# Gated values summed on VectorE head by head, in place of products on VectorE and sums on GpSimd

## The chip, the cores and the metric

The kernel runs on one core of one Trainium2 chip. The metric is the device time of one execution in microseconds (us), from the first to the last instruction and what lies around it. The engines are called as in the profile: PE is TensorE, DVE is VectorE, ACT is ScalarE, POOL is GpSimd, SP is SyncE.

## The reference

A stream x of 8 sequences of 512 tokens with 128 columns passes four layers, each added to the stream: attention with 16 heads, a mixture attention, another attention, and the same mixture again. Only the mixture's values matter here. It has 8 heads of 64 columns, and 5 experts; each head of each token picks two experts for its values:

```
gl_v = (x @ Ws).reshape(b, t, h, e)
wv = _topk_mask(gl_v, SEL) * jax.nn.sigmoid(gl_v)
xv = jnp.einsum('btd,edk->btek', x, Wv)
v = jnp.einsum('bthe,btek->bhtk', wv, xv)
scores = jnp.einsum('bhid,bhjd->bhij', q * scale, k)
probs = jax.nn.softmax(scores, axis=-1)
attn = jnp.einsum('bhij,bhjd->bihd', probs, v)
```

So the value of one head and token is a sum over the five experts of a gate times 64 columns that all heads share.

## The kernel before, in words

The two layers of each kind and the 8 sequences give 16 units of work. `iteration(j)` runs 19 times; it works on three units at once: unit j is prepared (normalised, projected), unit j-1 goes through attention A, and unit j-2 through the mixture F, whose last part falls into the iteration after. An iteration has 8 slots (0 to 3 for the four groups of attention heads, 4 to 7 for the four pairs of mixture heads) of up to 10 steps each; (slot, b) names a step. Each engine runs the same list of slots and steps in order, and semaphores (`Signal`) connect them. There is no planner: what stands at which step is written out by hand, in tables.

In slots 2 to 5 PE computes the scores of the mixture (L484), two of 512 columns at a time, into three banks S1a, S1b and S1c. For each, DVE takes the negative maximum (nmaxF, L991), and ACT the exponential (Pq, L805), which frees the bank for PE. Beside it, PE transposes or multiplies into S2 and ACT copies to PT; POOL masks PT in slots 0 to 3 (L1246).

The values of the mixture lie in `Vf` (128 tokens of each of NT = 4 token tiles i, 8 heads, 64 columns). They come from `xv` (the five experts' columns of a token tile) and the gates `wv_s`. `f_value_product(i, e)` (L1067) runs on DVE at the 20 steps of `V_STEPS` (L186), in the order of i and then e: one product of 512 columns for all eight heads (L1076), with both inputs spread by stride 0. For e = 0 it goes straight to `Vf`; for e = 1 to 4 it goes to one of four buffers in `ztmp`, and `f_value_sum` (L1264) on POOL adds it to `Vf` (L1271). `v_mult` counts products, `v_acc` counts sums. A product waits for the sum four before it, where the buffers go round. The last iteration with values, j = 17, has no attention beside it; there the steps are those of `V_LAST` (L189) and the buffers lie in `PT`.

PE reads `Vf` in slot 5 (`values`, L517, matmul L550), after a wait for the sums of the token tile. Four steps on other lines play a part: `rotate` (L954 and L960, DVE), `rest1` and `part2` (L1257 and L1261, POOL, which split the rotated tensor), and the sum of the residual with a bias into `res` (L1301, POOL), which stands at step (4, 8) behind DMA loads. `split_maxima` (L1004 and L1006, DVE) makes `nmb` at the start of slots.

Of the kernel before, what the change touches and what calls it, by code (L numbers as in the profile page):

```python
# [19 lines left out]
def attention_and_mixture(nc, x, wa, wp, ba, bv, bp, tab, wqk, wgv, wo, ident_in, mask_in, out):  # L20
# [47 lines left out]
    NF_B = GF * NT  # L68

    ctx = ExitStack()  # L70
    with ctx:
# [6 lines left out]
        class Signal:  # L78
# [76 lines left out]
        maskf = ztmp[:, 0, 0, 0:2, :].rearrange("p a b -> p (a b)")  # L155
        VBUF = 4
        vtmp = ztmp[:, :, :, :, :].rearrange("p b t e d -> p (b t e d)")[:, 0:VBUF * HF * DF].rearrange(
            "p (j h d) -> p j h d", j=VBUF, h=HF)
        S1 = [pb("S1a"), pb("S1b"), pb("S1c")]
# [79 lines left out]
        sig_e = Signal("sig_e", 1)  # L239
        v_mult = Signal("v_mult", NT * E)  # L240
        v_acc = Signal("v_acc", NT * (E - 1))
        z_mult = Signal("z_mult", HF)
# [62 lines left out]
        def mix_step(k, g, h):  # L305

            return (2, 5) if (k, g, h) == (UNITS + 1, 3, 1) else ((SA + g + 2) % NS, 2 * h + 1)

        def vtmp_of(k, n):

            return PT[:, n % VBUF // 2, NF_B + n % 2, :].rearrange("p (h d) -> p h d", h=HF) if k == UNITS + 1 else vtmp[:, n % VBUF, :, :]

# [111 lines left out]
        def _(pe):  # L424
# [7 lines left out]
            def iteration(j, a, f, f_end, a_prep, f_prep):  # L432
# [84 lines left out]
                def values(slot, kt):  # L517
# [26 lines left out]
                    else:  # L544
                        if kt == 0:
                            pe.wait_ge(exps_done.sem, exps_done.at(j, BEFORE2[slot]))
                        if group == SA:
                            pe.wait_ge(v_acc.sem, v_acc.at(j, (E - 1) * (kt + 1), 2))
                        for h in range(GF):
# [221 lines left out]
        def _(act):  # L771
# [6 lines left out]
            def iteration(j, a, f, f_end, a_prep, f_prep):  # L778
# [54 lines left out]
                def f_gates(i):  # L833
                    use = f"F gate{i}"
                    if i == 0:
                        act.wait_ge(v_mult.sem, v_mult.at(j, v_mult.per, 2))
                    act.wait_ge(*filled(j, use))
                    nc.scalar.activation(gate[:, :, i, :], bank(use)[:, 0:NG].rearrange("p (e g) -> p e g", e=E), ACT.Copy)
                    nc.scalar.activation(xv[:, i, :], bank(use)[:, NG:NG + NX], ACT.Copy).then_inc(is_free(use), 1)
# [66 lines left out]
        def _(dve):  # L906
            for s in (m0_drained, m1_drained, s1_read, maxF_ready, resA_ready, resF_ready, varA_ready, varF_ready, xnA_ready,
                      xnF_ready, rot_ready, nmb_ready, v_mult, z_mult, lnA_chain, lnF_chain, maxA_chain,
                      normA_chain, pick_chain, mix_chain):

                skipped = (M0_USES.index("A xnT") if s is m0_drained else M1_USES.index("A q") if s is m1_drained
                           else BEFORE1[2] if s is s1_read else 0)
                dve.sem_inc(s.sem, s.first + skipped)
# [11 lines left out]
            def iteration(j, a, f, f_end, a_prep, f_prep):  # L925
# [141 lines left out]
                def f_value_product(i, e):  # L1067
                    if i == 0 and e == 0:
                        dve.wait_ge(pick_chain.sem, pick_chain.at(j, 6, 2))
                        dve.wait_ge(y_filled.sem, y_filled.at(j, 1))  # L1070
                    if i == 0 and e == 1 and j <= UNITS:
                        dve.wait_ge(z_acc.sem, z_acc.at(j, HF - 1, 3))
                    n = i * (E - 1) + e
                    if e and n > VBUF:
                        dve.wait_ge(v_acc.sem, v_acc.at(j, n - VBUF, 2))
                    nc.vector.tensor_tensor(  # L1076
                        vtmp_of(j, n) if e else Vf[:, i, :, :],
                        xv[:, i:i + 1, e * DF:(e + 1) * DF].broadcast_to([P, HF, DF]),
                        wv_s[:, e, i, :].unsqueeze(2).broadcast_to([P, HF, DF]), ALU.mult).then_inc(v_mult.sem, 1)

# [11 lines left out]
                def f_mix(g, h, lag):  # L1092
# [133 lines left out]
        def _(pool):  # L1226
            for s in (rstdA_ready, rstdF_ready, outA_chain, rest1_ready, part2_ready, masked, v_acc, z_acc):
                pool.sem_inc(s.sem, s.first)
# [8 lines left out]
            def iteration(j, a, f, f_end, a_prep, f_prep):  # L1237
# [25 lines left out]

                def f_value_sum(i, e):  # L1264
                    if e == 0:
                        return
                    n = i * (E - 1) + e
                    pool.wait_ge(v_mult.sem, v_mult.at(j, i * E + e + 1, 2))
                    if n > 1:
                        pool.wait_ge(v_acc.sem, v_acc.at(j, n - 1, 2))  # L1270
                    nc.gpsimd.tensor_tensor(Vf[:, i, :, :], Vf[:, i, :, :], vtmp_of(j, n),  # L1271
                                            ALU.add).then_inc(v_acc.sem, 1)

                def f_mix(g, h, lag):
# [10 lines left out]
                for slot in range(NS):  # L1285
                    for b in range(STEPS):
# [11 lines left out]
                        if at == (4, 8) and a:  # L1298
# [78 lines left out]
```

## Time and profile before

| | us |
|---|---|
| runs (3): median | 1924.3 |
| runs: lowest and highest | 1922.47, 1925.94 |
| profiled execution, its own time | 1920.52 |
| profiled execution, span of its instructions | 1918.8 |

| engine | busy us | share | instructions |
|---|---|---|---|
| PE | 1762.0 | 92% | 11200 |
| DVE | 1591.7 | 83% | 2963 |
| ACT | 1261.8 | 66% | 2774 |
| POOL | 1041.5 | 54% | 1124 |

The granted TensorE clock is 0.987 of full speed over the span. Busy time counts a moment once, though instructions of one engine overlap a little; the mean time of an instruction includes that overlap. The start of an instruction less the start of the one before it is what the one before takes of its engine. The chain that ended last is followed back from the last instruction, at each step to what released it.

### The profile page before, as it was taken

To read this page: it belongs to the slowest core of one execution; us is meant where nothing else is said; L and a number is where in the kernel's file an instruction comes from. 1 tells how busy PE (TensorE), PEld (TensorE's weight loads), DVE (VectorE), ACT (ScalarE), POOL (GpSimd) and SP (SyncE) were. 2 spreads that over 40 slices of the span, in tenths; PEclk is the share of its full clock that TensorE was granted. 3 is DMA by queue.
4 is the path that set the end of the run, shared out by engine and by line. 5 is a ranking of instruction groups with operands and counts; after the bars stand their busy time and mean duration, and the time that the engine had idled before them with its cause. 6 is when DMAs were issued, how large, how long until landed. Compare 5 with 4: busy or idle time off the path is not lost.

```text
span 1918.8 us, 32180 instructions
## 1 busy us (share of the span) xinstructions
PE 1762.0 (92%) x11200; PEld 880.5 (46%) x11200; DVE 1591.7 (83%) x2963; ACT 1261.8 (66%) x2774; POOL 1041.5 (54%) x1124
## 2 busy tenths in 40 slices
PE   3779999999999999999999999999999999999997
PEld 1343545445454454545445454544545445354444
DVE  6587888989888898888889888898988889887775
ACT  1548577685766758576675767768576675857664
POOL 2426374664637456363755637466463755736453
PEclk8989999999999999999999999999999999999989
DMA  2211011111101111110111101111110111100000
GB/s 79 66 40 34 15 38 39 46 39 32 41 19 40 39 38 42 37 31 23 46 39 32 48 12 40 39 46 39 32 35 24 40 39 32 48 12 15 12 11 6
DMA packets 87375, 66.58 MB, mean 35 GB/s; under 512 B 10608, under 2 KB 82992, under 8 KB 87216
## 3 DMA queue, kind: packets, MB, share of 16 engines
q1 hardware_dynamic: 86400, 63.74, 10.9%
q8 instruction: 92, 1.51, 0.3%
q10 hardware_dynamic: 816, 0.79, 0.1%
q14 instruction: 67, 0.55, 0.1%
HBM read 30.42 MB, written 8.39 MB: 20 GB/s over the span
## 4 chain that ended last, share of the span: by engine, by line
PE 54%; DVE 33%; ACT 9%; issue 3%; POOL 0%; SPq 0%; DMA 0%; DVEq 0%; ACTq 0%; PEldq 0%; POOLq 0%
PE Y L550 10%; DVE nmaxA L986 7%; DVE nmaxF L991 5%; DVE ztmp L1104 5%; PE S2a L510 5%; PE S2b L510 4%; ACT Pq L805 4%; PE S1c L484 4%; PE S1b L484 4%; PE Y L540 3%; PE M L645 3%; DVE nmaxA L981 3%; PE M L603 3%; DVE ztmp L1076 3%; PE M L657 2%
## 5 line engine op out<-in xcount | busy, mean ns | idle before, releaser
L1281 POOL TENSOR_TENSOR Z<-Z,ztmp 128x1280 f32<-128x1280 f32 (+1 forms) x110 | 316.6, 2879 | 340.1 <-DVE ztmp L1104 339.6
L1246 POOL TENSOR_SCALAR_AFFINE_SELECT PT<-PT 128x256 f32<-128x256 f32 (+1 forms) x640 | 259.3, 416 | 279.0 <-ACT PT L790 274.2
L1271 POOL TENSOR_TENSOR Vf<-Vf,ztmp 128x512 f32<-128x512 f32 x240 | 318.1, 1325 | 83.8 <-DVE ztmp L1076 79.4
L790 ACT ACTIVATE PT<-S2a 128x512 f32<-128x512 f32 x320 | 191.7, 599 | 124.8 <-PE S2a L504 122.5
L550 PE MATMUL Y<-PT,Vf 128*64 128x512 f32 x1024 | 268.0, 614 | 0.0
L1076 DVE TENSOR_TENSOR ztmp<-xv,wv_s 128x512 f32<-128x512 f32 x240 | 244.3, 1018 | 0.0
L794 ACT ACTIVATE PT<-S2a 128x512 f32<-128x512 f32 x256 | 153.2, 599 | 129.1 <-PE S2a L510 125.6
L484 PE MATMUL S1c<-Kf,Qf 64*128 64x512 f32 x352 | 199.5, 647 | 33.9 <-ACT Pq L805 32.8
L484 PE MATMUL S1a<-Kf,Qf 64*128 64x512 f32 x352 | 198.9, 645 | 25.6 <-ACT Pq L805 25.6
L790 ACT ACTIVATE PT<-S2b 128x512 f32<-128x512 f32 x320 | 191.6, 599 | 25.8 <-PE S2b L504 25.6
L484 PE MATMUL S1b<-Kf,Qf 64*128 64x512 f32 x320 | 181.9, 649 | 13.2 <-ACT Pq L805 10.9
L1104 DVE TENSOR_TENSOR ztmp<-M,wz 128x1280 f32<-128x1280 f32 x110 | 162.6, 1480 | 20.7 <-PE M L578 20.7
L794 ACT ACTIVATE PT<-S2b 128x512 f32<-128x512 f32 x256 | 153.4, 599 | 38.0 <-PE S2b L510 33.6
L540 PE MATMUL Y<-PT,Vs 128*18 128x512 f32 (+3 forms) x2048 | 169.1, 438 | 1.3 <-PEq L494 1.3
L805 ACT ACTIVATE Pq<-S1c,nmaxF 128x512 f32<-128x512 f32 x176 | 120.7, 686 | 73.2 <-DVE nmaxF L991 73.2
L991 DVE TENSOR_REDUCE nmaxF<-S1c 128x1 f32<-128x512 f32 x176 | 120.4, 684 | 55.4 <-PE S1a L484 53.5
L510 PE MATMUL S2a<-ident,Pq 128*128 128x128 f32 x1024 | 162.1, 281 | 1.3 <-ACT Pq L805 1.3
L510 PEld LDWEIGHTS S2a<-ident,Pq 128*128 128x128 f32 x1024 | 107.9, 141 | 116.9 <-ACT PT L794 81.7
L991 DVE TENSOR_REDUCE nmaxF<-S1a 128x1 f32<-128x512 f32 x176 | 120.2, 683 | 47.1 <-PE S1b L484 45.2
L510 PE MATMUL S2b<-ident,Pq 128*128 128x128 f32 x1024 | 155.0, 274 | 4.4 <-ACT PT L790 4.4
L986 DVE TENSOR_REDUCE nmaxA<-S1b 128x1 f32<-128x128 f32 (+2 forms) x272 | 126.3, 493 | 30.9 <-PE S1b L474 30.9
L805 ACT ACTIVATE Pq<-S1a,nmaxF 128x512 f32<-128x512 f32 x176 | 121.6, 691 | 28.9 <-DVE nmaxF L991 28.9
(137 smaller groups left out, 3720.8 us busy)
## 6 DMA issues: line engine op xcount, KB each, us to landing
Qs<-parts SPq DMA_DIRECT2D x96, 128.0 KB
Ks<-parts SPq DMA_DIRECT2D x90, 128.0 KB
tab_s<-in_tab SPq DMA_DIRECT2D x16, 512.0 KB, 4.4
out_x<-res SPq DMA_DIRECT2D x31, 256.0 KB, 2.4
xr<-out_x SPq DMA_DIRECT2D x24, 256.0 KB, 3.0
wa_s<-in_wa SPq DMA_DIRECT2D x16, 320.0 KB, 3.2
xl<-in_x SPq DMA_DIRECT2D x8, 256.0 KB, 3.1
Qs<-mrowA SPq DMA_DIRECT2D x128, 4.0 KB, 1.7
```

The costliest lines, as they stand in the source:

```text
L484: nc.tensor.matmul(S1[(n - 1 + h) % len(S1)][:, :], Qf[own, pair, qt * P:qt * P + P], Kf[own, pair, :], start=True, stop=True).then_inc(s1 ...
L510: last = nc.tensor.transpose(t[:, kt * P:kt * P + P], Pq[:, slot % 2, b, kt * P:kt * P + P], ident[:, :])
L550: last = nc.tensor.matmul(Y[DF * h:DF * h + DF, :], Vf[:, kt, GF * (group - SA) + h, :], PT[:, group % 2, NT * h + kt, :], start=(kt == 0) ...
L790: nc.scalar.activation(PT[:, slot % 2, b, :], t[:, :], ACT.Exp, scale=SCALE_A).then_inc(exps_done.sem, 1)
L794: nc.scalar.activation(PT[:, slot % 2, NT * h:NT * h + NT, qt * P:qt * P + P], t[:, :].rearrange("p (k q) -> p k q", q=P), ACT.Copy).then_ ...
L805: nc.scalar.activation(Pq[:, g % 2, b, :], S1[(n - 1) % len(S1)][:, :], ACT.Exp, bias=nmaxF[:, GF * g + h, qt:qt + 1], accum_out=denF[:, q ...
L986: last = nc.vector.tensor_reduce(nmaxA[:, GA * group + h, qt:qt + 1], t[:, col:col + (qt + 1) * P], AX.X, ALU.max, negate=True)
L991: nc.vector.tensor_reduce(nmaxF[:, GF * (group - SA) + h, qt:qt + 1], t[:, :], AX.X, ALU.max, negate=True).then_inc(maxF_ready.sem, 1)
L1076: nc.vector.tensor_tensor(vtmp_of(j, n) if e else Vf[:, i, :, :], xv[:, i:i + 1, e * DF:(e + 1) * DF].broadcast_to([P, HF, DF]), wv_s[:, e ...
L1246: last = nc.gpsimd.affine_select(out=v, in_=v, compare_op=ALU.is_ge, fill=0.0, base=0, pattern=pattern, channel_multiplier=-1)
L1271: nc.gpsimd.tensor_tensor(Vf[:, i, :, :], Vf[:, i, :, :], vtmp_of(j, n), ALU.add).then_inc(v_acc.sem, 1)
L1281: nc.gpsimd.tensor_tensor(Z[:, own, :, :], Z[:, own, :, :], ztmp[:, hh % 2, own, :, :], ALU.add).then_inc(z_acc.sem, 1)
```

## The change

In `f_value_product` the product for e = 0 stays as it was. For e = 1 to 4 one instruction for each head takes its place: `scalar_tensor_tensor` multiplies the 64 columns of `xv` by the head's gate, one scalar per partition, and adds the 64 columns of `Vf`, in place. These eight instructions are called a block below. `f_value_sum` and the buffers fall away, and one signal, `v_done`, counts what is finished.

```diff
-        v_mult = Signal("v_mult", NT * E)
-        v_acc = Signal("v_acc", NT * (E - 1))
+        v_done = Signal("v_done", NT * E)
...
-                            pe.wait_ge(v_acc.sem, v_acc.at(j, (E - 1) * (kt + 1), 2))
+                            pe.wait_ge(v_done.sem, v_done.at(j, E * (kt + 1), 2))
...
-                        act.wait_ge(v_mult.sem, v_mult.at(j, v_mult.per, 2))
+                        act.wait_ge(v_done.sem, v_done.at(j, v_done.per, 2))
...
-                    if i == 0 and e == 1 and j <= UNITS:
-                        dve.wait_ge(z_acc.sem, z_acc.at(j, HF - 1, 3))
-                    n = i * (E - 1) + e
-                    if e and n > VBUF:
-                        dve.wait_ge(v_acc.sem, v_acc.at(j, n - VBUF, 2))
-                    nc.vector.tensor_tensor(
-                        vtmp_of(j, n) if e else Vf[:, i, :, :],
-                        xv[:, i:i + 1, e * DF:(e + 1) * DF].broadcast_to([P, HF, DF]),
-                        wv_s[:, e, i, :].unsqueeze(2).broadcast_to([P, HF, DF]), ALU.mult).then_inc(v_mult.sem, 1)
+                    if e == 0:
+                        nc.vector.tensor_tensor(
+                            Vf[:, i, :, :], xv[:, i:i + 1, 0:DF].broadcast_to([P, HF, DF]),
+                            wv_s[:, 0, i, :].unsqueeze(2).broadcast_to([P, HF, DF]), ALU.mult).then_inc(v_done.sem, 1)
+                        return
+
+                    dve.wait_ge(v_done.sem, v_done.at(j, i * E + e, 2))
+                    for h in range(HF):
+                        last = nc.vector.scalar_tensor_tensor(Vf[:, i, h, :], xv[:, i, e * DF:(e + 1) * DF], wv_s[:, e, i, h:h + 1],
+                                                              Vf[:, i, h, :], ALU.mult, ALU.add)
+                    last.then_inc(v_done.sem, 1)
...
-                    if hh == 1:
-                        dve.wait_ge(v_acc.sem, v_acc.at(j, v_acc.per, lag))
...
-                def f_value_sum(i, e):
-                    if e == 0:
-                        return
-                    n = i * (E - 1) + e
-                    pool.wait_ge(v_mult.sem, v_mult.at(j, i * E + e + 1, 2))
-                    if n > 1:
-                        pool.wait_ge(v_acc.sem, v_acc.at(j, n - 1, 2))
-                    nc.gpsimd.tensor_tensor(Vf[:, i, :, :], Vf[:, i, :, :], vtmp_of(j, n),
-                                            ALU.add).then_inc(v_acc.sem, 1)
...
-                        if at in v_steps(j) and f:
-                            f_value_sum(*divmod(v_steps(j).index(at), E))
```

On DVE the places stay. These are the rows of slot 4, from the e = 1 product of token tile 2 at step (4, 1) on, before:

```order
L1076 TENSOR_TENSOR ztmp<-xv,wv_s 128x512
L991 TENSOR_REDUCE nmaxF<-S1c 128x1
L991 TENSOR_REDUCE nmaxF<-S1a 128x1
L1076 TENSOR_TENSOR ztmp<-xv,wv_s 128x512
L991 TENSOR_REDUCE nmaxF<-S1b 128x1
L1076 TENSOR_TENSOR ztmp<-xv,wv_s 128x512
L991 TENSOR_REDUCE nmaxF<-S1c 128x1
L1076 TENSOR_TENSOR ztmp<-xv,wv_s 128x512
L991 TENSOR_REDUCE nmaxF<-S1a 128x1
L1076 TENSOR_TENSOR Vf<-xv,wv_s 128x512
L991 TENSOR_REDUCE nmaxF<-S1b 128x1
```

The same place with the change:

```order
L1071 SCALAR_TENSOR_TENSOR Vf<-xv,wv_s,Vf 128x64 x8
L983 TENSOR_REDUCE nmaxF<-S1c 128x1
L983 TENSOR_REDUCE nmaxF<-S1a 128x1
L1071 SCALAR_TENSOR_TENSOR Vf<-xv,wv_s,Vf 128x64 x8
L983 TENSOR_REDUCE nmaxF<-S1b 128x1
L1071 SCALAR_TENSOR_TENSOR Vf<-xv,wv_s,Vf 128x64 x8
L983 TENSOR_REDUCE nmaxF<-S1c 128x1
L1071 SCALAR_TENSOR_TENSOR Vf<-xv,wv_s,Vf 128x64 x8
L983 TENSOR_REDUCE nmaxF<-S1a 128x1
L1064 TENSOR_TENSOR Vf<-xv,wv_s 128x512
L983 TENSOR_REDUCE nmaxF<-S1b 128x1
```

Each product for e = 1 to 4 is now eight instructions in the same gap between reductions; nothing else on DVE has moved.

On POOL, the end of slot 3 to slot 5 of the same iteration, from a mask on, before:

```order
L1246 AFFINE_SELECT PT<-PT 128x128
L1271 TENSOR_TENSOR Vf<-Vf,ztmp 128x512
L1246 AFFINE_SELECT PT<-PT 128x2x128 x2
L1257 TENSOR_TENSOR rotated<-rotated,parts 128x512
L1271 TENSOR_TENSOR Vf<-Vf,ztmp 128x512
L1261 TENSOR_TENSOR parts<-rotated,parts 128x512
L1271 TENSOR_TENSOR Vf<-Vf,ztmp 128x512 x4
L1301 TENSOR_TENSOR res<-xr,bp_s 128x512
L1271 TENSOR_TENSOR Vf<-Vf,ztmp 128x512 x3
L1252 TENSOR_TENSOR rstd<-var_eps,minus_half 128x4
```

and with the change:

```order
L1238 AFFINE_SELECT PT<-PT 128x128
L1238 AFFINE_SELECT PT<-PT 128x2x128 x2
L1249 TENSOR_TENSOR rotated<-rotated,parts 128x512
L1253 TENSOR_TENSOR parts<-rotated,parts 128x512
L1283 TENSOR_TENSOR res<-xr,bp_s 128x512
L1244 TENSOR_TENSOR rstd<-var_eps,minus_half 128x4
```

The residual's sum (`res`) now stands right behind the last split of the keys, with no sum of values ahead of it or behind it.

## Rows read from the trace of the kernel before

**Rows 1.** The page: busy time of the engines, and shares of the chain that ended last.

```profile
PE 1762.0 (92%) x11200; PEld 880.5 (46%) x11200; DVE 1591.7 (83%) x2963; ACT 1261.8 (66%) x2774; POOL 1041.5 (54%) x1124
...
PE 54%; DVE 33%; ACT 9%; issue 3%; POOL 0%; SPq 0%; DMA 0%; DVEq 0%; ACTq 0%; PEldq 0%; POOLq 0%
```

**Rows 2.** Busy time by stretch, slots 2 to 5 of a middle iteration: last stretch, sum.

```profile
1093.00:1108.00 15.00, 13.65 (x91) 7.38 (x91) 14.87 (x23) 11.38 (x28) 12.43 (x9) 1.00 0.17 54
sum 53.00, PE 48.27 PEld 22.11 DVE 44.18 ACT 41.70 POOL 36.23; mean PE 12.07 PEld 5.53 DVE 11.04 ACT 10.43 POOL 9.06
```

**Rows 3.** The chain in order of time, same iteration: start us, us, engine, tensor, line.

```profile
1072.21 1.33 DVE ztmp L1076
...
1093.61 0.89 DVE ztmp L1076
```

**Rows 4.** Groups by line, POOL: shapes xcount | busy us, mean ns | idle before, releasers.

```profile
L1271 POOL TENSOR_TENSOR Vf<-Vf,ztmp 128x512 f32<-128x512 f32 x240 | 318.1, 1325 | 83.8 <-DVE ztmp L1076 79.4 <-POOL Vf L1271 0.4
```

**Rows 5.** Groups by line, DVE, same columns.

```profile
L1076 DVE TENSOR_TENSOR ztmp<-xv,wv_s 128x512 f32<-128x512 f32 x240 | 244.3, 1018 | 0.0
...
L1076 DVE TENSOR_TENSOR Vf<-xv,wv_s 128x512 f32<-128x512 f32 x64 | 55.2, 862 | 0.0
...
L954 DVE SCALAR_TENSOR_TENSOR rotated<-M,ba_s,tab_s 128x512 f32<-128x512 f32 x62 | 46.2, 745 | 34.2 <-PE M L603 34.1
...
L1006 DVE TENSOR_TENSOR nmb<-nmaxA,nmb 128x16 bf16<-128x16 f32 x64 | 29.9, 467 | 2.2
...
L1165 DVE TENSOR_TENSOR res<-M,xr 128x512 f32<-128x512 f32 x15 | 10.2, 681 | 3.1 <-PE M L698 3.1
...
L1038 DVE TENSOR_TENSOR rotated<-gate 128x64 bf16<-128x64 f32 x16 | 3.5, 218 | 0.0
```

**Rows 6.** One line's instructions: duration ns min/median/max, first and last start us.

```profile
L1006 DVE TENSOR_TENSOR nmb<-nmaxA,nmb x64: 174/180/1270, 42.9 to 1739.1; 128x16 bf16<-128x16 f32 x64
```

**Rows 7.** Timeline, DVE, gate comparisons: start us, us, engine, line, operation, tensors.

```profile
1015.79 0.22 DVE L1038 TENSOR_TENSOR rotated<-gate 128x64 bf16<-128x64 f32 x1
1015.92 0.48 DVE L1035 TENSOR_TENSOR rotated<-gate 128x320 bf16<-128x320 f32 x1
```

**Rows 8.** Timeline, DVE, slots 2 to 4; in brackets the idle time before, and releaser.

```profile
1058.38 0.68 DVE L1076 TENSOR_TENSOR ztmp<-xv,wv_s 128x512 f32<-128x512 f32 x1
1058.98 0.68 DVE L1165 TENSOR_TENSOR res<-M,xr 128x512 f32<-128x512 f32 x1
1059.89 0.69 DVE L991 TENSOR_REDUCE nmaxF<-S1b 128x1 f32<-128x512 f32 x1 [0.23 <-PE S1c L484]
...
1063.15 0.69 DVE L991 TENSOR_REDUCE nmaxF<-S1a 128x1 f32<-128x512 f32 x1 [1.38 <-PE S1b L484]
...
1072.14 1.41 DVE L1076 TENSOR_TENSOR ztmp<-xv,wv_s 128x512 f32<-128x512 f32 x1
...
1078.12 0.69 DVE L991 TENSOR_REDUCE nmaxF<-S1c 128x1 f32<-128x512 f32 x1 [1.38 <-PE S1a L484]
...
1081.44 0.69 DVE L991 TENSOR_REDUCE nmaxF<-S1b 128x1 f32<-128x512 f32 x1 [0.31 <-PE S1c L484]
...
1086.13 0.69 DVE L991 TENSOR_REDUCE nmaxF<-S1a 128x1 f32<-128x512 f32 x1 [1.35 <-PE S1b L484]
...
1089.84 0.69 DVE L991 TENSOR_REDUCE nmaxF<-S1c 128x1 f32<-128x512 f32 x1 [0.47 <-PE S1a L484]
...
1092.91 0.69 DVE L991 TENSOR_REDUCE nmaxF<-S1b 128x1 f32<-128x512 f32 x1 [1.19 <-PE S1c L484]
```

**Rows 9.** Timeline, POOL, same iteration, same columns.

```profile
1071.85 1.15 POOL L1257 TENSOR_TENSOR rotated<-rotated,parts 128x512 f32<-128x512 f32 x1
...
1100.85 1.72 POOL L1301 TENSOR_TENSOR res<-xr,bp_s 128x512 f32<-128x512 f32 x1
```

**Rows 10.** By stretch, L1076 alone, DVE (count): slots 4 to 5; the last iteration.

```profile
1093.00:1107.00 14.00, 8.80 (x7) 1.00 0.18 57
1858.00:1876.00 18.00, 13.18 (x11) 1.00 0.04 12
```

More of the change, by code:

```diff
@@ L155, in attention_and_mixture @@
         maskf = ztmp[:, 0, 0, 0:2, :].rearrange("p a b -> p (a b)")
-        VBUF = 4
-        vtmp = ztmp[:, :, :, :, :].rearrange("p b t e d -> p (b t e d)")[:, 0:VBUF * HF * DF].rearrange(
-            "p (j h d) -> p j h d", j=VBUF, h=HF)
         S1 = [pb("S1a"), pb("S1b"), pb("S1c")]
@@ L307, in mix_step @@
             return (2, 5) if (k, g, h) == (UNITS + 1, 3, 1) else ((SA + g + 2) % NS, 2 * h + 1)
-        def vtmp_of(k, n):
-            return PT[:, n % VBUF // 2, NF_B + n % 2, :].rearrange("p (h d) -> p h d", h=HF) if k == UNITS + 1 else vtmp[:, n % VBUF, :, :]
         def steps_of_output(k):
@@ L907, in _ @@
             for s in (m0_drained, m1_drained, s1_read, maxF_ready, resA_ready, resF_ready, varA_ready, varF_ready, xnA_ready,
-                      xnF_ready, rot_ready, nmb_ready, v_mult, z_mult, lnA_chain, lnF_chain, maxA_chain,
+                      xnF_ready, rot_ready, nmb_ready, v_done, z_mult, lnA_chain, lnF_chain, maxA_chain,
                       normA_chain, pick_chain, mix_chain):
@@ L1226, in _ @@
         def _(pool):
-            for s in (rstdA_ready, rstdF_ready, outA_chain, rest1_ready, part2_ready, masked, v_acc, z_acc):
+            for s in (rstdA_ready, rstdF_ready, outA_chain, rest1_ready, part2_ready, masked, z_acc):
                 pool.sem_inc(s.sem, s.first)
```

## The prediction

> **What bounds the kernel now.** First the busy shares and the chain that ended last [rows 1]: PE is busy 92% of the span, DVE 83%, and the chain lies on PE for 54% and on DVE for 33%. So neither engine is the bound everywhere; they take turns. Which of them has the turn where the change acts is read from the busy time by stretch in a middle iteration [rows 2]. From 1055 to 1108 us, slots 2 to 5, where 16 of an iteration's 20 products run that the change touches (from e = 1 up), DVE works 44.2 of 53 us and so has 8.8 us of idle time; in the last stretch of it, 1093 to 1108 us, it works 14.87 of 15 us. The idle time lies in pieces ahead of reductions that wait for PE [rows 8], and in slots 4 and 5 there is almost none. The chain agrees: at 1072.2 and at 1093.6 us it runs over a DVE product itself [rows 3]. So a longer product is free where a wait for PE follows it, and costs its full length where DVE is the one that is waited for.
>
> **What is removed.** 256 POOL sums; 240 of them take 318.1 us [rows 4]. POOL is not on the chain, so their time itself gives nothing. They give two things to DVE. A DVE product with both inputs in SBUF loses time when a POOL instruction that reads SBUF runs: the product at 1072.14 takes 1.41 us [rows 8] while POOL's subtraction runs from 1071.85 to 1073.00 [rows 9], where an undisturbed one takes 0.68. On average the ztmp product takes 1.018 and the Vf product 0.862 us [rows 5]. And nmb, a 16-column subtraction, takes 0.467 us on average [rows 5] against a median of 0.18 [rows 6]; the long ones, up to 1.27, wait for a sum. The waits that vanish (for ztmp's four buffers, for the sums' end, for Z) cost nothing in the waits view, and are taken at nothing; DVE was not late through them, and POOL's masks, which now run earlier, were waited for by nobody.
>
> **What is added.** 256 blocks of 8 instructions, 2048 in all, on DVE. None of this form (two SBUF tensors, one scalar per partition, 64 columns) is in the trace, so it is built up. Consecutive DVE instructions overlap: a 64-column product that takes 0.218 us starts at 1015.79, and the next starts at 1015.92, 0.13 later [rows 7]. A 512-column one of 0.68 us is followed after 0.60, an overlap of 0.08 (1058.38 and 1058.98, [rows 8]). What the scalar per partition costs: the rotation, which has one, takes 0.745 us against 0.681 for a sum of the same size from PSUM without one, 0.064 more [rows 5]. So one instruction holds DVE for 0.13 + 0.065 = 0.195 us, a block for 8 x 0.195 = 1.56, say **1.55 us**, in place of 0.94 (1.018 less 0.08) on average, or of 0.60 where POOL did not disturb. From below a block is 8 x 0.13 = 1.04 us, if the scalar's read hides under the instruction before; from above 8 x (0.218 + 0.065) = 2.26, if nothing overlaps. I take 1.55: the rotation is the one large group of this operation with a scalar per partition, and the gate comparisons are the group of this size.
>
> The Trainium skill (VectorE: DVE Perf Modes, "The DRAIN you can't avoid") says that the next DVE instruction does not start until the pipe is empty. By that the block is the upper bound, and the sum would be that of rival 3; the starts 0.13 us apart speak against it here.
>
> **Where it lands, in a middle iteration** (times from [rows 8]; an undisturbed product grows by 1.55 - 0.60 = 0.95; one that meets a POOL instruction that stays also grows by 0.95).
> - Start of slot 2: nmb, which waits for a sum there, gives back up to 1.27 - 0.18 = 1.09, the block of (1,9) takes 0.95: nothing. The three of slot 2 stand ahead of waits for PE, of 0.23 and 1.38 us for the first two, and the reductions' results are wanted later than they come: nothing.
> - (3,0), on the chain: **+0.95**.
> - (3,2): followed by 1.38 us of waiting, nothing. (3,4): 0.95 less 0.31 of waiting leaves 0.64, which (3,7) takes along: 0.64 + 0.95 - 1.35 = 0.24.
> - (4,1): 0.24 + 0.95 less 0.47 of waiting: **+0.72**. (4,3): hidden in 1.19 us of waiting.
> - (4,4) to (5,2), seven products without a wait between: they take 8.80 us, less 7 x 0.08 of overlap, 8.24 [rows 10]. Six become blocks and the one for e = 0 falls to 0.60: 6 x 1.55 + 0.60 = 9.90. **+1.66**.
> - POOL's res sum (1.72 us, [rows 9]) comes earlier, since seven sums no longer stand ahead of it, and falls into these blocks; such meetings cost a product 0.73 (1.41 - 0.68), and nothing if POOL slips in beside a reduction from PSUM. I take **+0.6**.
>
> Together 0.95 + 0.72 + 1.66 + 0.6 = 3.9 us; 15 such iterations give 59 us. In the last one with products (its own step table) eleven products stand in one DVE chain from 1858 to 1876 us: 13.18 us less 11 x 0.08 is 12.30; nine blocks and two of 0.60 give 15.15, **+2.9**. The wait of a block for the one before it costs only where no reduction stands between, twice there, 0.08 of lost overlap each: nothing elsewhere. Sum: 62 us. The profiled execution took 1920.5 us of which 1918.8 are the span, so 1982; it lies 3.8 us below the median of the runs shown, so **1986 us** against 1924.3, 3.2% slower.
>
> **Rivals.**
> 1. *Faster: the scalar's read is hidden.* Then a block is 1.04 us and shorter than what the disturbed products took. The seven products cost 6 x 1.04 + 0.60 - 8.24 = -1.40, (3,0) +0.44, the others are hidden, and res costs 0 to 0.6: -0.4 to -1.0 us per iteration, and the tail 9 x 1.04 + 1.2 - 12.30 = -1.7. That is -7 to -16 us, about 1912. It decides at a block of 1.10 us, 0.138 us per instruction. For it: the starts 0.13 apart, and the disturbance by POOL that goes. Against it: 0.064 us for the scalar in the rotation, which stands in the same queue. The Trainium skill (VectorE: DVE Perf Modes, "The TRN2 errata") counts 58 cycles beside the columns at 0.96 GHz, an estimate of 127 ns for 64 columns, and names no price for a scalar: by it this rival would hold.
> 2. *No cover: DVE sets the pace from slot 1 to 5.* The waits for PE are parts of loops (product, reduction, exponential, next S1), and if PE shifts with DVE they stay open and hide nothing. Then all the added work lands: 16 x (1.55 - 0.94) = 9.8, less 4 x (0.862 - 0.68) = 0.7 for e = 0 and 4 x (0.467 - 0.18) = 1.1 for nmb, plus 0.6: 8.6 us per iteration, 129 + 2.9 in all, 2056. For it: the 8.8 us of idle time are only just as long as the added work. Against it: three of the six waits named above exceed 0.95 by far.
> 3. *The instructions of a block do not overlap*, since each reads and writes Vf beside the one before: 2.26 us per block. The added work is 16 x (2.26 - 0.94) - 1.8 + 0.6 = 19.9 us, more than the 8.8 idle; what is over, 11.1 us, times 15, and 9.2 in the tail: 176, so 2100. Against it: the overlap in the gate comparisons, which also write one tensor one after the other.
> 4. *No change*: a block near 1.1 us by a scalar that is partly hidden.
>
> **How the numbers follow.** The forecast 0.68, rival 1 0.08, rival 2 0.14, rival 3 0.06, rival 4 0.04. Measured against the 1924.3 us, less than 0.2% (3.8 us) can hardly be told from no change. Forecast, rivals 2 and 3 are slower by more than that: 0.88; rival 4 is the same: 0.04; rival 1 is faster: 0.08. Within the forecast the time runs from about 1940 (res hidden, (4,1) hidden, the scalar at 0.05 us) up to rival 2. The range is 1940 to 2058: it leaves out rivals 1, 3 and 4, 0.18.
>
> **What the next profile would show.** The new group: 2048 instructions of about 0.28 us, busy time 256 x 1.6 = about 420 us; eight starts about 0.195 us apart. If they are 0.13 apart, rival 1; if 0.28, rival 3. The Vf product of e = 0 falls from 0.862 towards 0.70, nmb from 0.467 towards 0.2; POOL's busy time falls by about 340 us, and nobody waits for its masks. In 1093 to 1108 us and its like DVE stays busy throughout, and the stretch is longer by some 2 to 3 us; ACT's waits for nmaxF grow by that. The idle pieces after (3,2), (3,7) and (4,3) shrink; if they are as long as before and the iteration has grown by 8 us, it is rival 2. The forecast is wrong in its size if the block is right and the iteration's growth is not near 4 us.

## The result, and the profile after

The changed kernel takes **2008.1 us** (median of 4 runs, 2007.3 to 2010.2) against 1924.4 us: 1.043 times as long, 95% interval 1.0417 to 1.0444. The forecast was 1986 us, 3.2% slower, with a range to 2058: right in direction, and 22 us short. The profiled execution has a span of 2006.9 us, 88.1 more than before; the medians are 83.6 apart, since the profiled execution of before lies 3.9 us under its median and that of after 0.6 above.

Where do the 88 us lie? The start of the product for e = 0 of each token tile is a mark that both kernels have. Read off the DVE timelines, the first mark comes 2.65 us later (141.06 against 138.41); the 15 iterations from there to the first mark of the last iteration with values take 1779.8 against 1699.7 us, **5.34 us more each, 80.1 in all**; from that mark to the end it is 86.1 against 80.7, 5.4 more. Inside a middle iteration (medians of the 15):

| from one mark to the next, us | forecast | before | after | more |
|---|---|---|---|---|
| tile 0 to 1 (slot 2) | +0 | 17.85 | 18.39 | +0.54 |
| tile 1 to 2 (slot 3) | +1.19 | 16.02 | 17.21 | +1.19 |
| tile 2 to 3 (slot 4) | | 9.95 | 12.80 | +2.85 |
| tile 3 to the next iteration (slots 4 and 5, the rest) | | 70.30 | 71.06 | +0.76 |
| the last two together | +2.74 | | | +3.61 |

The forecast's +1.19 is 0.95 at (3,0) and the 0.24 that it has left behind (3,7), which lies ahead of the mark of tile 2; its +2.74 is the rest of 3.93.

The page of after, busy time and the shares of the chain that ended last, which answer to [rows 1]:

```profile
PE 1789.8 (89%) x11200; PEld 896.3 (45%) x11200; DVE 1776.1 (88%) x4755; ACT 1265.7 (63%) x2774; POOL 691.8 (34%) x868
...
DVE 45%; PE 43%; ACT 7%; issue 4%; DMA 0%; SPq 0%; POOL 0%; DVEq 0%; ACTq 0%; PEldq 0%; POOLq 0%
```

DVE works 184.4 us more and the span grew by 88.1, so something less than half of the added work shows as time and the rest was covered. The chain runs over DVE for 45% of the span, where it was 33%. POOL's work fell by 349.7 us; it stood on the chain for 0% [rows 1], so that time itself gave nothing.

Groups by line of after (columns as in [rows 4]), which answer to [rows 5]; then one line's instructions, as in [rows 6]:

```profile
L1071 DVE SCALAR_TENSOR_TENSOR Vf<-xv,wv_s,Vf 128x64 f32<-128x64 f32 x2048 | 477.5, 301 | 0.1
...
L1064 DVE TENSOR_TENSOR Vf<-xv,wv_s 128x512 f32<-128x512 f32 x64 | 46.5, 726 | 0.0
...
L1283 POOL TENSOR_TENSOR res<-xr,bp_s 128x512 f32<-128x512 f32 x16 | 20.7, 1297 | 0.0
L998 DVE TENSOR_TENSOR nmb<-nmaxA,nmb 128x16 bf16<-128x16 f32 x64 | 13.6, 213 | 2.2
```

```profile
L1071 DVE SCALAR_TENSOR_TENSOR Vf<-xv,wv_s,Vf x2048: 264/274/1306, 143.3 to 1964.2; 128x64 f32<-128x64 f32 x187
```

An instruction of a block takes 0.274 us in the median, as forecast (0.28). But 477.5 us over 256 blocks is 1.87 us of busy time for a block, where the forecast had 1.6. The product for e = 0 fell from 0.862 to 0.726, nmb from 0.467 to 0.213, both as forecast.

The DVE timeline of after, first a block of slot 2 and one of slot 3, then slot 4, and under it POOL's, answer to [rows 8] and [rows 9]:

```profile
1105.12 1.79 DVE L1071 SCALAR_TENSOR_TENSOR Vf<-xv,wv_s,Vf 128x64 f32<-128x64 f32 x8
...
1119.46 2.51 DVE L1071 SCALAR_TENSOR_TENSOR Vf<-xv,wv_s,Vf 128x64 f32<-128x64 f32 x8
...
1133.05 1.65 DVE L1071 SCALAR_TENSOR_TENSOR Vf<-xv,wv_s,Vf 128x64 f32<-128x64 f32 x8
1134.65 0.69 DVE L983 TENSOR_REDUCE nmaxF<-S1a 128x1 f32<-128x512 f32 x1
1135.26 0.68 DVE L1064 TENSOR_TENSOR Vf<-xv,wv_s 128x512 f32<-128x512 f32 x1
1135.86 0.68 DVE L983 TENSOR_REDUCE nmaxF<-S1b 128x1 f32<-128x512 f32 x1
1136.46 2.55 DVE L1071 SCALAR_TENSOR_TENSOR Vf<-xv,wv_s,Vf 128x64 f32<-128x64 f32 x8
...
1140.13 1.64 DVE L1071 SCALAR_TENSOR_TENSOR Vf<-xv,wv_s,Vf 128x64 f32<-128x64 f32 x8
1141.85 0.69 DVE L983 TENSOR_REDUCE nmaxF<-S1b 128x1 f32<-128x512 f32 x1
1142.46 2.91 DVE L1071 SCALAR_TENSOR_TENSOR Vf<-xv,wv_s,Vf 128x64 f32<-128x64 f32 x8
1145.29 0.68 DVE L983 TENSOR_REDUCE nmaxF<-S1c 128x1 f32<-128x512 f32 x1
```

```profile
1105.98 0.47 POOL L1238 TENSOR_SCALAR_AFFINE_SELECT PT<-PT 128x256 f32<-128x256 f32 x1 [2.53 <-ACT PT L782]
...
1119.17 1.15 POOL L1249 TENSOR_TENSOR rotated<-rotated,parts 128x512 f32<-128x512 f32 x1
...
1136.49 1.26 POOL L1249 TENSOR_TENSOR rotated<-rotated,parts 128x512 f32<-128x512 f32 x1
...
1141.72 1.16 POOL L1253 TENSOR_TENSOR parts<-rotated,parts 128x512 bf16<-128x512 f32 x1 [3.97 <-ACT parts L815]
1142.84 1.27 POOL L1283 TENSOR_TENSOR res<-xr,bp_s 128x512 f32<-128x512 f32 x1
```

A block that meets nothing takes 1.64 us and holds DVE for 1.60 (1133.05 to the reduction at 1134.65). The block at 1136.46 meets the split of POOL's at 1136.49 and takes 2.55. The block at (4, 4), at 1142.46, meets the end of another split and the whole of the residual's sum, and takes 2.91. That block stands on the chain, here in order of time (start us, us, what):

```profile
1141.87 0.67 DVE nmaxF L983
1142.54 2.83 DVE Vf L1071 x8
1145.37 0.60 DVE nmaxF L983
1145.97 1.56 DVE Vf L1071 x8
1147.53 0.61 DVE nmaxF L983
...
1148.17 0.79 ACT Pq L797 x2
```

ACT waits for these reductions and PE for ACT. From the waits view of after (us in total, times, longest):

```profile
ACT Pq L797 <- DVE nmaxF L983: 191.4, 187, 4.1
...
PE S1c L476 <- ACT Pq L797: 85.5, 51, 4.2
```

and of before:

```profile
ACT Pq L805 <- DVE nmaxF L991: 114.3, 146, 2.9
...
PE S1c L484 <- ACT Pq L805: 32.8, 48, 1.3
```

The PE timeline at the end of that chain:

```profile
1149.09 0.66 PE L476 MATMUL S1c<-Kf,Qf 64*128 64x512 f32 x1 [2.83 <-ACT Pq L797]
...
1150.69 1.12 PE L570 MATMUL M<-ident,ySB 128*128 128x128 f32 x4
```

And the busy time by stretch (columns as in [rows 2]: PE, PEld, DVE, ACT, POOL, then the granted TensorE clock, the DMA share, GB/s):

```profile
1135.00:1149.00 14.00, 9.98 (x74) 4.43 (x72) 13.92 (x42) 10.51 (x26) 4.06 (x4) 1.00 0.35 113
1149.00:1152.00 3.00, 2.91 (x14) 2.06 (x15) 3.00 (x13) 2.67 (x6) 0.00 (x0) 0.77 0.00 1
1152.00:1155.00 3.00, 3.00 (x14) 1.42 (x13) 2.97 (x14) 1.42 (x4) 0.00 (x0) 0.66 0.00 0
1155.00:1160.00 5.00, 5.00 (x30) 2.57 (x29) 4.75 (x21) 3.28 (x9) 0.00 (x0) 1.00 0.00 0
sum 55.00, PE 46.41 PEld 20.01 DVE 52.77 ACT 41.19 POOL 14.09; mean PE 7.74 PEld 3.33 DVE 8.80 ACT 6.86 POOL 2.35
```

From 1105 to 1160 us (the sum has two earlier rows) DVE is idle for 2.2 of 55 us, where it was 8.8 of 53 [rows 2]: most of the pieces that were to hide blocks are used up. And after PE's wait of 2.83 us the granted clock falls between 1149 and 1155 us from 2.4 to 1.2 GHz, for some 3 us. The kernel before shows a clock of 1.00 at this place in every middle iteration; after shows the fall there in all of them.

### The profile page after: what moved, and what is told of

Its sections match the earlier page's. It is cut to its first block, busy times and chain, and to the rows that moved or that the text cites. A ratio compares the mean times of both kernels' runs of the same rounds, so it can differ in the third digit from the quotient of the medians.

```text
span 2006.9 us, 33475 instructions
## 1 busy us (share of the span) xinstructions
PE 1789.8 (89%) x11200; PEld 896.3 (45%) x11200; DVE 1776.1 (88%) x4755; ACT 1265.7 (63%) x2774; POOL 691.8 (34%) x868
## 4 chain that ended last, share of the span: by engine, by line
DVE 45%; PE 43%; ACT 7%; issue 4%; DMA 0%; SPq 0%; POOL 0%; DVEq 0%; ACTq 0%; PEldq 0%; POOLq 0%
DVE Vf L1071 10%; DVE nmaxA L978 8%; PE Y L542 8%; DVE nmaxF L983 6%; DVE ztmp L1096 6%; PE S1c L476 5%; PE S2a L502 4%; PE S2b L502 4%; ACT Pq L797 4%; DVE nmaxA L973 3%; PE Y L532 2%; PE M L649 2%; PE S1b L476 2%; DVE beaten_by L1042 2%; ACT PT L782 2%
## 5 line engine op out<-in xcount | busy, mean ns | idle before, releaser
L1071 DVE SCALAR_TENSOR_TENSOR Vf<-xv,wv_s,Vf 128x64 f32<-128x64 f32 x2048 | 477.5, 301 | 0.1
L1238 POOL TENSOR_SCALAR_AFFINE_SELECT PT<-PT 128x256 f32<-128x256 f32 (+1 forms) x640 | 245.8, 394 | 498.9 <-ACT PT L782 495.9
L476 PE MATMUL S1c<-Kf,Qf 64*128 64x512 f32 x352 | 211.6, 683 | 86.6 <-ACT Pq L797 85.5
L476 PE MATMUL S1b<-Kf,Qf 64*128 64x512 f32 x320 | 188.5, 671 | 10.8 <-ACT Pq L797 8.7
L502 PE MATMUL S2b<-ident,Pq 128*128 128x128 f32 x1024 | 161.0, 281 | 10.4 <-ACT PT L782 10.4
L1244 POOL TENSOR_TENSOR rstd<-var_eps,minus_half 128x4 f32<-128x4 f32 x32 | 32.6, 1019 | 345.3 <-DVE var_eps L927 345.3
L978 DVE TENSOR_REDUCE nmaxA<-S1c 128x1 f32<-128x384 f32 (+2 forms) x240 | 113.1, 498 | 24.6 <-PE S1c L466 24.6
```

Of the source, the lines that this page charges most:

```text
L476: nc.tensor.matmul(S1[(n - 1 + h) % len(S1)][:, :], Qf[own, pair, qt * P:qt * P + P], Kf[own, pair, :], start=True, stop=True).then_inc(s1 ...
L502: last = nc.tensor.transpose(t[:, kt * P:kt * P + P], Pq[:, slot % 2, b, kt * P:kt * P + P], ident[:, :])
L978: last = nc.vector.tensor_reduce(nmaxA[:, GA * group + h, qt:qt + 1], t[:, col:col + (qt + 1) * P], AX.X, ALU.max, negate=True)
L1071: last = nc.vector.scalar_tensor_tensor(Vf[:, i, h, :], xv[:, i, e * DF:(e + 1) * DF], wv_s[:, e, i, h:h + 1], Vf[:, i, h, :], ALU.mult, A ...
L1238: last = nc.gpsimd.affine_select(out=v, in_=v, compare_op=ALU.is_ge, fill=0.0, base=0, pattern=pattern, channel_multiplier=-1)
```

## The experiments

Theory: the block costs what was forecast, 0.195 us an instruction, and the time is lost where blocks, lengthened by POOL, stand ahead of reductions that ACT waits for. Rivals: the number of DVE instructions or its total decides, or the same loss comes with any sum on DVE. Each ratio below is against runs of the kernel before made beside the experiment's (medians 1927.1 us for 1 to 4, 1926.5 for 5 to 8, 1923.6 for 9 and 10).

**1. The gate's scalar.**

```diff
-    last = nc.vector.scalar_tensor_tensor(Vf[:, i, h, :], xv[:, i, e * DF:(e + 1) * DF], wv_s[:, e, i, h:h + 1],
+    last = nc.vector.scalar_tensor_tensor(Vf[:, i, h, :], xv[:, i, e * DF:(e + 1) * DF], 1.5,
                                           Vf[:, i, h, :], ALU.mult, ALU.add)
```

> The gate of the eight instructions of a block is replaced by the constant 1.5, so no scalar per partition is read; this leaves the gates of experts 1 to 4 out of the result. My theory: the scalar's read costs 0.065 us of each instruction and DVE is the engine waited for in slots 3 to 5. Then eight starts are 0.13 us apart, an undisturbed block shows 1.12 us (1.64 with the scalar), and about nine of the sixteen shortened blocks of an iteration stand on the path: 9 x 0.52 x 15 = 70 us less, about 1935 us (1915 to 1950). Rival: the price is the number of instructions, or the scalar hides and something else fills the 0.195 us: blocks of 1.6 us and no time under 2000 us.

Measured: 1951.0 us, 1.0125 times the time before [1.0109, 1.014].

```profile
L1071 DVE SCALAR_TENSOR_TENSOR Vf<-xv,Vf x2048: 202/214/1307, 142.1 to 1904.2; 128x64 f32<-128x64 f32 x187
```

The median fell from 274 to 214 ns: the scalar per partition costs 0.06 us an instruction, as read from the rotation. With what follows from it (the falls of the clock in slot 4 are gone too) it is worth 57 us of the change's 84. But even with blocks of 1.16 us the kernel is 24 us slower than before, where rival 1 of the forecast had put the break-even at a block of 1.10: something besides the length of an undisturbed block costs. The block at (4, 4) still meets the residual's sum, and takes 2.54 in place of 1.16:

```profile
1110.74 2.54 DVE L1071 SCALAR_TENSOR_TENSOR Vf<-xv,Vf 128x64 f32<-128x64 f32 x8
```

**2. The residual's sum later.** GpSimd's sum into `res` waits until the tile's last value is done; no DVE instruction changes.

```diff
                             pool.wait_ge(resF_stored.sem, resF_stored.at(j, 1, 3))
+                            if f:
+                                pool.wait_ge(v_done.sem, v_done.at(j, v_done.per, 2))
                             nc.gpsimd.tensor_tensor(res[:, :, :], xr[:, :, :],
```

> POOL's residual sum waits until the last block of the iteration is done, so it no longer falls between the blocks of slot 4. My theory: POOL's meeting there makes the block at step (4, 4) 2.9 us long instead of 1.64 to 2.4, PE then waits 2.8 us, and the granted clock falls to 1.2 GHz for 3 to 4 us behind it. Without it the block at (4, 4) is 2.1 us at most, PE's wait shrinks by 0.8 or more, and the time falls by 10 to 30 us, to 1978 to 1998; if the clock stays up in the middle iterations, at the lower end. Rival: the meeting is absorbed and the clock's fall covered by DVE's chain: within 4 us of 2008.

Measured: 1991.3 us, 1.0333 [1.0318, 1.0349], 17 us less than after. The block at (4, 4) now:

```profile
1130.90 1.88 DVE L1071 SCALAR_TENSOR_TENSOR Vf<-xv,wv_s,Vf 128x64 f32<-128x64 f32 x8
```

1.88 in place of 2.91 (it still meets the split's end), and slot 4 falls by the same 1.03 us, from 12.80 to 11.77: the meeting with `res` is 1.0 us of each iteration. PE's wait there falls from 2.83 to 1.80 us and is the same in each iteration. What follows it is not. Two iterations of this one kernel, PE timeline and clock by stretch:

```profile
309.49 0.66 PE L476 MATMUL S1c<-Kf,Qf 64*128 64x512 f32 x1 [1.80 <-ACT Pq L797]
...
311.08 0.66 PE L570 MATMUL M<-ident,ySB 128*128 128x128 f32 x4
...
1136.50 0.66 PE L476 MATMUL S1c<-Kf,Qf 64*128 64x512 f32 x1 [1.80 <-ACT Pq L797]
...
1138.10 1.11 PE L570 MATMUL M<-ident,ySB 128*128 128x128 f32 x4
```

```profile
310.00:313.00 3.00, 2.42 (x18) 1.52 (x16) 3.00 (x15) 2.70 (x7) 0.00 (x0) 1.00 0.14 45
...
1137.00:1140.00 3.00, 3.00 (x17) 1.99 (x13) 3.00 (x14) 2.36 (x6) 0.00 (x0) 0.67 0.13 46
```

At 309 us the clock stays at 2.4 GHz, at 1136 us it falls to 1.2. Of the first thirteen, iterations in which it stays take 70.4 or 70.5 us from the mark of tile 3 to the next iteration, those in which it falls 71.0 to 71.4. So **one fall costs 0.5 to 1.0 us** here, all instructions being the same. It need not cost anything: in experiment 6, where PE waits 1.92 us there, the clock falls in seven of twelve iterations (the second to the thirteenth), and these take 71.3 or 71.4 us where the others take 71.3.

**3. One block per pair of reductions.** Only the table of steps changes.

```diff
-        V_STEPS = [(s, b) for s, bs in ((1, (8, 9)), (2, (1, 3, 5, 8)), (3, (0, 2, 4, 7)), (4, (0, 1, 3, 4, 5, 6, 7)),
-                                        (5, (0, 1, 2)))
+        V_STEPS = [(s, b) for s, bs in ((1, (8, 9)), (2, (1, 3, 5, 8)), (3, (0, 2, 4, 6, 8)), (4, (1, 3, 5, 7, 8)),
+                                        (5, (0, 2, 4, 6)))
```

> Only the table of steps changes: at most one block between two score pairs of PE, so no two blocks stand back to back (slot 4: steps 1, 3, 5, 7, 8; slot 5: 0, 2, 4, 6). The work is the same. My theory: the time is lost where two blocks meet in one pair (steps 4 and 5 of slot 4, 0 and 1 of slot 5) and where POOL meets them; a block alone fits into a pair of 3.1 us (two reductions of 0.6 and 1.56). Then the iteration falls from 119.5 to about 116, PE has no wait of 2.8 us and the clock does not fall: 1950 to 1980 us. Rival (no cover): DVE is the bound from slot 1 to 5 whatever the place of its work: 2000 us or more.

Measured: 2018.6 us, 1.0476 [1.0459, 1.0494], slower than after: a miss. DVE, and the ACT instruction that waits for it:

```profile
1138.24 0.69 DVE L952 TENSOR_TENSOR rotated<-rotated 128x512 f32<-128x512 f32 x1
1138.85 1.73 DVE L1071 SCALAR_TENSOR_TENSOR Vf<-xv,wv_s,Vf 128x64 f32<-128x64 f32 x8
1140.50 0.68 DVE L983 TENSOR_REDUCE nmaxF<-S1c 128x1 f32<-128x512 f32 x1
```

```profile
1141.21 0.69 ACT L797 ACTIVATE Pq<-S1c,nmaxF 128x512 f32<-128x512 f32 x1 [2.44 <-DVE nmaxF L983]
```

The block moved to (3, 6) stands right behind the rotation, ahead of a reduction that was already late: ACT waits 2.44 us. PE's longest wait in a middle iteration is 1.68 us here and the clock falls in only three of them, nearly as the theory had said, and the kernel is slower all the same; so it is not by those two that it loses. Spreading blocks evenly is not the point; what stands ahead of a late reduction is, as these rows suggest. No run moves this block alone.

**4. Product and sum on DVE, as two instructions of 512 columns.** The kernel before, its sums moved from GpSimd to VectorE, each one step behind its product.

```diff
+        DVE_TILES = (0, 1, 2, 3,)
...
+                    nc.vector.tensor_tensor(Vf[:, i, :, :], Vf[:, i, :, :], vtmp_of(j, n),
+                                            ALU.add).then_inc(v_acc.sem, 1)
...
+                            for k in (nth - 1, nth):
+                                if k >= 0 and k % E and k // E in DVE_TILES and (k < nth or k == NT * E - 1):
+                                    f_value_sum(*divmod(k, E))
```

> The kernel before with POOL's sums moved to DVE: a product of 512 columns and, one step later, a sum of 512 columns, two instructions of 0.6 us in place of a block of 1.56; same result, POOL as free as in the changed kernel. My theory (DVE's holding time decides): against before the seven products of slots 4 and 5 take 6 x 1.2 + 0.6 = 7.8 us instead of 8.2, step (3, 0) grows by 0.6, the rest is mostly hidden: 0 to 1.5 us per iteration, so 1920 to 1950 us, some 65 us less than the changed kernel. Rival: what costs is that the sums run on DVE at all and POOL's other instructions disturb them: 1985 us or more.

Measured: 1979.2 us, 1.0271 [1.0256, 1.0287]: between the two, so both were wrong. An undisturbed pair holds DVE for 1.20 us (2 x 0.60), 0.4 less than a block, and still the kernel is 52 us slower than before. The sum at (4, 4) meets `res`; DVE and POOL:

```profile
1128.78 1.75 DVE L1086 TENSOR_TENSOR Vf<-Vf,ztmp 128x512 f32<-128x512 f32 x1
```

```profile
1128.27 1.71 POOL L1313 TENSOR_TENSOR res<-xr,bp_s 128x512 f32<-128x512 f32 x1
```

**5 and 6. Blocks in some token tiles only.** The other tiles keep the product on VectorE and the sum on GpSimd.

```diff
+        BLOCK_TILES = (0,)
...
+                    if e and i in BLOCK_TILES:
+                        dve.wait_ge(v_mult.sem, v_mult.at(j, i * E + e, 2))
+                        for h in range(HF):
...
```

> Blocks for the first token tile alone (steps (1, 9) to (2, 5), 4 of the 16), products and POOL's sums for the other three as before. Against before, the stretch up to the second tile is 0.56 us longer in the changed kernel. My theory as it stands now: DVE's added time fills its waits for PE first, and here there are waits, so about 15 x 0.5 = 8 us over before: 1930 to 1940 us. Rival (added time lands whole, wherever it stands): 4 blocks, each 0.85 to 0.95 longer, 3.5 us per iteration, 50 us: 1970 to 1985 us.

> Blocks for the last two token tiles alone (steps (4, 1) to (5, 2), 8 of the 16), the first two as before. POOL still waits at each of these steps, so its residual sum comes at its old place. My theory: these eight stand where DVE has no waits left; in the changed kernel the stretches there grew by 2.84 + 0.79 us per iteration. Without the residual sum's meeting some 1.0 less: 2.0 to 3.5 us per iteration, 30 to 55 us over before, plus up to 5 in the last iteration: 1957 to 1985 us. Rival (each block costs the same everywhere): half of the changed kernel's 83 us, about 1969 us, and the first tile's run then shows 20 us.

Measured: tile 0 alone (4 of 16 blocks) 1930.2 us, 1.0018 [1.0008, 1.0027]; tiles 2 and 3 alone (8 of 16) 1978.0 us, 1.0262 [1.0247, 1.0278]. Over the 64 blocks of the one that is 3.5 us, 0.05 a block; over the 128 of the other 50 us, 0.4 a block. That rules out a plain count of instructions. It is not cover alone: the blocks of 6 average 1.92 us, since three of eight in an iteration meet POOL's remaining work, those of 5 1.73. In 5 the stretch of slot 2 still grows, from 17.85 to 18.30: it is not quite free.

**7. Experiment 4 with the residual's sum later** (the added wait is that of experiment 2, on `v_acc`).

> Product and sum of 512 columns on DVE as in the run before, with POOL's residual sum behind the last of them. My theory: in that run the sum at (4, 4) meets the residual sum and takes 1.75 us instead of 0.68, PE then waits 2.2 us, and the clock falls to 1.2 GHz behind it. Without the meeting 1.1 us go at once and the fall with them, another 0.5 to 1.2: 24 to 35 us less than 1979: 1944 to 1955 us. Rival: the meeting and the fall are hidden: within 5 us of 1979.

Measured: 1954.5 us, 1.0142 [1.0127, 1.0157], 25 us less than 4. Slot 4 falls by 1.08 us, and the stretch from the mark of tile 3 to the next iteration from 71.0 to 71.4 (in 4, from the second iteration on) to 70.2: there the clock no longer falls. In slot 3 it falls more often than in 4 (12 iterations against 8), which takes some 5 us of the gain back at 1.3 us a fall.

**8. GpSimd sums tiles 0 and 1, VectorE tiles 2 and 3, the residual's sum later.**

```diff
+        DVE_TILES = (2, 3,)
```

> Products and POOL's sums for the first two token tiles as before, where DVE waits for PE; products and sums on DVE for the last two, where POOL's sums made each product longer (seven products 8.24 us before, 6 x 1.2 + 0.6 = 7.8 now); the residual sum behind them. My theory: within a microsecond per iteration of before, 1915 to 1940 us. Rival (any DVE work more is paid): 8 sums of 0.6 us, 4.8 less the 3.2 that the products lose, 1.6 us per iteration, about 1950 us.

Measured: 1936.6 us, 1.0047 [1.0032, 1.0062]: within the theory's range and still slower than before. Slot 4 takes 10.67 us against 9.95.

**9. Blocks dealt out again, and the residual's sum later.** The step (3, 7), which had cover, is kept.

```diff
-        V_STEPS = [(s, b) for s, bs in ((1, (8, 9)), (2, (1, 3, 5, 8)), (3, (0, 2, 4, 7)), (4, (0, 1, 3, 4, 5, 6, 7)),
-                                        (5, (0, 1, 2)))
+        V_STEPS = [(s, b) for s, bs in ((1, (8, 9)), (2, (1, 3, 5, 8)), (3, (0, 2, 4, 7, 9)), (4, (1, 3, 5, 7, 8)),
+                                        (5, (0, 1, 2, 4)))
```

> The changed kernel with two edits: GpSimd's sum of the residual waits until VectorE has finished that tile's values, and the blocks of VectorE are dealt to other steps: slot 3 at steps 0, 2, 4, 7, 9, slot 4 at 1, 3, 5, 7, 8, slot 5 at 0, 1, 2, 4. Theory (a block costs 1.55 us of VectorE wherever it stands, and what hurts is two of them, or one that meets GpSimd's sum of the residual, ahead of the reduction that ScalarE waits for): 1958 to 1985 us, about 1970, no wait of TensorE above 2 us in slot 4, and a granted clock of 0.98 or more over the whole span. Rival (VectorE's total busy time decides, not where the blocks stand): 1988 us or more, as with the later sum of the residual alone (1991).

Measured: 1981.6 us, 1.0299 [1.0285, 1.0313], the upper edge of the theory's range and only 6 us under the rival's 1988, so this run alone hardly tells the two apart; no wait of PE over 2 us in slot 4, and the clock stays up in slots 4 and 5 of every middle iteration:

```profile
1123.00:1138.00 15.00, 13.34 (x92) 6.76 (x85) 14.63 (x57) 12.01 (x31) 1.16 (x1) 1.00 0.17 54
1138.00:1153.00 15.00, 13.81 (x90) 7.96 (x89) 12.71 (x42) 9.67 (x21) 2.29 (x2) 1.00 0.06 19
```

So with no fall of the clock, and no meeting with `res`, the change still costs 3%: the larger part lies with the blocks themselves, at their length and with the masks and splits that they still meet (1.80 us a block on average).

**10. A candidate.** GpSimd keeps the sums of tiles 1 and 2, VectorE takes tiles 0 and 3 (two instructions; a tile's last sum right behind its product), the residual's sum later.

```diff
+        DVE_TILES = (0, 3)
```

> The kernel before, with the sum of the residual made later and the sums of values split by tile: VectorE makes product and sum of tiles 0 and 3 itself (as two instructions over all heads), GpSimd keeps the sums of tiles 1 and 2. Theory (GpSimd's sums of the first and last tile stand in the way of other work, those of the middle tiles are hidden): the stretches from one tile's first product to the next take about 17.6, 16.0, 10.0 and 17.9 us against 17.85, 16.02, 9.95 and 17.96 before, 5 us or so less over 15 iterations and the tail: 1915 to 1924 us, a little faster than before. Rival (every sum that VectorE takes on costs its own 0.5 us in slot 4, where no slack is left): 1930 us or more.

Measured: 1922.3 us, 0.999 [0.998, 0.9999], inside the theory's range but not to be told from no change. The 15 iterations take 3.7 us less in its profile (1696.0 against 1699.7), and its start 5.3 us more (first mark at 143.68). No version here beats the kernel before by more than a measurement can tell.

## Why the prediction was right, and 22 us short

**What was right.** "One instruction holds DVE for 0.13 + 0.065": 0.195 us. An undisturbed block holds DVE for 1.60 to the next reduction, 1.55 was said, and experiment 1 takes the 0.06 of the scalar out alone. Rival 3 (no overlap, 2.26) is thereby out. Of the section of the Trainium skill that the prediction names on this (VectorE: DVE Perf Modes, "The DRAIN you can't avoid") it gives only a part: the section says too that a next instruction which is not held starts earlier. The trace agrees with that: instructions of a block are 0.274 us long and start 0.196 us apart (eight of them end after 1.64). The place was right too: slot 2 costs least, slots 4 and 5 most (experiments 5 and 6).

**Rival 1** fell twice over: the scalar's read is not hidden, and where it is taken away the kernel is still slower. But for (3,0) and `res`, the forecast counted the disturbance by POOL as gone with the sums. It is not: POOL's masks, splits and residual sum stay, and a block of 1.6 us meets them more often than a product of 0.6. Blocks average 1.87 us, 0.23 over the undisturbed 1.64.

**The sum, term by term,** per middle iteration:
- *Slot 2, "nothing"*: measured +0.54 (experiment 5, those blocks alone: +0.45). The step that failed is that "the reductions' results are wanted later than they come". The trade at the start of the slot came out (nmb fell from 1.26 to 0.18 on the chain). But the block at (2, 1) takes 1.79, since it meets a mask of POOL's (at 1105.98), and only 0.23 of waiting stood behind it. The reduction that waited there comes 1.0 us later behind the mark than before, ACT and PE wait for it, and the block is now on the chain.
- *(3, 0) "+0.95", and 0.24 left behind (3, 7)*: +1.19 in slot 3, as forecast. The block at (3, 0) meets the split, as its product had, and takes 2.51 against 1.41, 1.1 more; the others of the slot leave 0.1.
- *(4, 1), the seven in a row and `res`, "+0.72" (0.48 without what slot 3 left), "+1.66", "+0.6"*, 2.74 in all: measured +3.61. In it `res` is 1.03 by experiment 2, not 0.6: the forecast took the disturbance of a short product (0.73), where a block can be held for most of POOL's instruction. The fall of the clock, which the forecast did not have, is about 0.6, an estimate from experiment 2 (71.06 here; 70.4 or 70.5 in those iterations of it in which the clock stays up). That leaves about 2.0 for the blocks, where 2.14 was said.

So 1.4 us more than forecast in each of 15 iterations, 21 us, come from slot 2 (0.54), `res` (0.43) and the clock (0.6), less 0.16 of blocks that were hidden better than thought. The clock's part is some 9 us in all.

**The last iteration, "+2.9"**, measured +5.4. From the product at (4, 4) to the reduction behind the last one, the chain that the forecast counted, it takes 21.5 us against 17.3, 4.1 more; 1.0 of that is a wait for PE that before does not have there, behind a stretch at 1.2 GHz (1952.7 to 1959.5 us):

```profile
1962.22 0.69 DVE L983 TENSOR_REDUCE nmaxF<-S1a 128x1 f32<-128x512 f32 x1 [1.03 <-PE S1b L476]
```

Another 1.6 us lie ahead of that chain, at the blocks of the first two token tiles, which the forecast left out. In experiment 1 all from the mark to the end takes 80.6 us, no longer than before.

**The start, +2.65**, was in no term; no changed instruction stands ahead of that mark: see below. With it the profiles are 26 us further apart than forecast, the medians 22, for the reason given at the top.

**Rival 2** (DVE sets the pace, 8.6 us per iteration) did not happen: covers hid more than half of DVE's added 184.4 us. But its warning was just: the idle time left is 2.2 us, and the truth lies between the forecast and it. (Against it the forecast names six waits; it had listed seven.)

**POOL's masks**, "waited for by nobody": that reading was wrong, if without weight. PE's weight loads stand idle behind masks for 10.0 us in all before, and for 6.5 after.

On the meetings the Trainium skill (SBUF — State Buffer, "SBUF: two separate sides") says that a DVE instruction with two SBUF inputs and a GpSimd one that reads SBUF lock each other out of a shared pair of ports for a whole instruction. The trace agrees: in the block at 1142.46 one of the eight, at 1142.89, takes 1.31 us in place of 0.27, while the residual's sum runs from 1142.84 to 1144.11.

## What to carry to other kernels

Moving an accumulation to the engine that makes the product frees an engine that was not the bound, and pays with the one that was. Before fusing a wide product and its sum into many narrow instructions, multiply the start-to-start time of the narrow ones (the fixed part plus 0.06 us for a scalar per partition, here) by their count, and look which reductions stand behind them that someone is late for. And look at what the removed work had been holding back: the residual's sum, freed to come early, fell on a block ahead of a late reduction and cost 17 us until it was made to wait.

## What was not expected of the hardware

**The same wait, two clocks.** In experiment 2 the same wait of PE (1.80 us, same place, same instructions ahead) is followed by the full clock in some iterations and by half of it in others. Experiments 4 and 7 show it in slot 3, behind a wait of 2.19 us in each iteration: in 4, the iterations alternate from the second on, 17.8 us with the fall and 16.5 without, 1.3 us for one fall. Behind after's 2.83 us in slot 4 it fell in every iteration, and behind a wait of 1.98 us at the same place in experiment 1, longer than that of experiment 2, in none. So the length of the wait alone does not tell. The Trainium skill (TensorE: Matmul & The Clock Gate, "Part 1: The HAM clock gate") says that the watch on the engine's activity does not start with the kernel; the alternation agrees with that, and no run here shows more of its cause.

**The start.** Long before the first block, PE waits 1.35 us in each kernel ahead of the same 32 matmuls. Before:

```profile
86.37 2.35 PE L540 MATMUL Y<-PT,Vs 128*18 128x512 f32 x32 [1.35 <-PEq L494]
```

and after:

```profile
86.00 3.84 PE L532 MATMUL Y<-PT,Vs 128*18 128x512 f32 x32 [1.35 <-PEq L486]
```

After, the clock fell there (0.71 from 84 to 88 us; 1.00 before), and experiment 10 shows it too (3.85 us). Their first marks come 2.65 and 5.3 us late, and the second of these alone is more than the 0.2% that was taken as the least to be told. Over the twelve kernels the first mark lies between 137.7 and 143.7 us, though the same instructions stand ahead of it (603 matmuls, 224 of DVE); the mean granted clock up to it is 0.89 in the two earliest (before and experiment 8) and 0.85 to 0.88 in the others. With one profile of each, whether this belongs to the program or to the execution is not shown; executions of the kernel before alone took 1919.7 to 1928.9 us. A difference of that size wants marks inside the program, or many runs.
